# Turned attention scores over 99 rows of the array in place of 128, and no rows of zeros under the queries

## The chip, the cores and the metric

The kernel runs on one core of one Trainium2 chip. The metric is device time of one execution in microseconds (us). Before the change the median of three runs is 1045.04 us, the lowest 1035.89 and the highest 1047.79.

## The reference, cut to what matters

Two decoder-like layers work on `x` (16 sequences, 112 rows, 256 features) with a context of 375 rows for each sequence. The first layer is a masked cross attention with layer norms and a mixture of experts. The second layer is the one that the change touches: a cross attention with 16 heads of 16 features, without a mask, and a small linear layer behind it.

```python
def _L1_xattn_ref(queries, keys, values, Wq, Wk, Wv, Wo):
    q = split_heads(queries @ Wq.T)          # 16 sequences, 16 heads, 112 x 16
    k = split_heads(keys @ Wk.T)             # 16 sequences, 16 heads, 375 x 16
    v = split_heads(values @ Wv.T)
    scores = einsum('bhqd,bhkd->bhqk', q, k) * scale
    attn = softmax(scores, axis=-1)
    ctx = einsum('bhqk,bhkd->bhqd', attn, v)
    return ctx ... @ Wo.T
x = x + _L1_xattn_ref(_layernorm(x), ctx_1024, ctx_1024, ...)
x = x + _L1_ffn_ref(_layernorm(x), W, b, V_r, C)
```

## The kernel before, in words

The first layer and its experts fill the span up to about 650 us; nothing in them is touched. Then comes `layer1`. It treats the 16 sequences ("batches", `b`) one behind the other, in groups of four (`i`), and each batch has 16 heads.

Queries and keys are each cut into three bf16 parts whose sum is nearly the f32 value. Six products of parts are enough, and six blocks of 16 features lie under one another, so that one matmul over `DEPTH` = 96 rows gives the score of one head. The keys of a batch lie in `kst` (128 rows, four slots of batches, 16 heads, 378 places), and the queries of a group in `qst` (128 rows, two slots of groups, 16 heads, 448 places). Both come by DMA from DRAM (`load_keys`, `load_queries` on ScalarE's queue).

Each score is computed twice. `scores` multiplies the queries (stationary, 96 x 112) by the keys (moving, 96 x 375), and VectorE reads only the row maxima out of it (`maximum`, L1472). The negated maxima are cut into three bf16 parts, turned over by the TensorE (`maxima_T`, L1719), copied to `mT` by VectorE (L1491) and written by SyncE's DMAs (`maxima`, L1346) into rows 96, 97 and 98 of `qst`. `transposed` (L1733) then computes the turned scores with the maximum already taken off: the stationary operand is a piece of `kst` with 128 keys, the moving one the 112 queries of a head, and rows 96 to 98 of `kst` hold ones, so that the three parts of the negated maximum are added by the matmul itself. ScalarE takes the exponential (`exps`, L1619), and `outputs` (L1741) multiplies by the values.

`transposed` takes all 128 rows of both tensors. Rows 99 to 127 of `qst` must therefore hold zeros and rows 96 to 127 of `kst` ones. ScalarE fills them: `under_keys(slot)` (L1589) for the four slots of keys and `below_queries(slot)` (L1593) for the two slots of queries. Each is one activation over 32 partitions. The order on ScalarE is written out by hand: 

```python
under_keys(0)
below_queries(0)
turned_over("q", 0)
queries(0)
scaled(1, range(G))
store_queries(0)
load_queries(0)
below_queries(1)
for slot in range(1, 4):
    under_keys(slot)
```

After these come the batches. SyncE's `maxima(b)` waits for the copy `mT` and for `below0` or `below1`, the semaphores of the two fills of `qst`. TensorE waits for the maxima's rows and for `under0` to `under3` before the turned scores of a batch. The stream of TensorE is also fixed by hand: while batch b is being turned and multiplied by values, the plain scores of batch b + 2 are interleaved with it, two heads at a time, each pair behind VectorE's maximum of the pair before.

Of the kernel before, what the change touches and what calls it, by code (L numbers as in the profile page):

```python
# [13 lines left out]
ACT = mybir.ActivationFunctionType  # L14

P = 128
B, S, D = 16, 112, 256
K = 375
KC = 125
NKC = K // KC  # L20
KP = (NKC - 1) * KC + P
# [3 lines left out]
GS = G * S  # L25
E, SE, H = 8, 2, 512
HM = H // P
NH, HD = 16, 16
# [1231 lines left out]
def layer1(nc, ctx, dram, out, x_res, weight1, weight2, slots, ps, bank, ident, ones, always, new_semaphore):  # L1260
# [5 lines left out]
    def sem(name):  # L1266
        return new_semaphore(name)

    DEPTH = 3 * 2 * HD
    QUAD = 4  # L1270
    yscr, kscr, vscr, qscr = (dram[n] for n in ("yscr", "kscr", "vscr", "qscr"))
    wq1 = sb("wq1", [P, C, D])
    wo1 = sb("wo1", [P, C, D])
# [13 lines left out]
    kst = sb("kst", [P, 4, NH, KP], BF16)  # L1287
    qst = sb("qst", [P, 2, NH, GS], BF16)
# [11 lines left out]

    s = {n: sem("d_" + n) for n in (
        "weights_in", "y_in0", "y_in1", "y_in2", "y_in3", "wf_ps", "wf_ready", "identb_ready", "under0", "under1", "under2", "under3",
        "below0", "below1", "dve", "pool", "half_ready", "scaled", "added", "mixed", "mv_ready", "rstd_ready", "xh_ready",
        "xT_ps", "xT_ready", "q_ps", "q1_ready", "q_read", "q2_ready", "q3_ready", "q_out", "qs_in0", "qs_in1",
        "k_in0", "k_in1", "k_in2", "k_in3", "v_in0", "v_in1", "s_ps", "s_max", "m_ready", "mT_ps", "mT_ready",
        "mrow_in0", "mrow_in1", "st_ps", "p_ready", "pv_ps", "outT_ready", "out_ps", "heads_ready", "o_ps", "x3_ready", "bf_added",
        "f_ps", "res_ready", "res_out0", "res_out1", "res_out2", "res_out3")}
# [23 lines left out]
    @block.sync  # L1331
    def _(sp):
        for dst, name in ((wq1, "wq1_t"), (wo1, "wo1_t"), (wf, "wf_t")):
            sp.dma_start(dst[:], dram[name].rearrange("(c p) n -> p c n", p=P)).then_inc(s["weights_in"], 16)
        for dst, name in ((vrT, "vr_t"), (cfT, "cf_t")):
            sp.dma_start(dst[:], dram[name]).then_inc(s["weights_in"], 16)

        sp.dma_start(bf_b[:], dram["bf"].rearrange("(o n) -> o n", o=1).to_broadcast([S, D])).then_inc(s["weights_in"], 16)

        def maxima(b):  # L1340
            i, j = divmod(b, G)
            sp.wait_ge(s["mT_ready"], b + 1)

            sp.wait_ge(s[f"below{i % 2}"], 1)
            for k in range(3):
                sp.dma_start(qst[DEPTH + k:DEPTH + k + 1, i % 2, :, j * S:(j + 1) * S], mT[k * NH:(k + 1) * NH, b % 2, :]).then_inc(s[f"mrow_in{b % 2}"], 16)  # L1346

        def results(i):
            for j in range(G):
                sp.wait_ge(s["res_ready"], i * G + (j + 1))  # L1350
                sp.dma_start(out[i * G + j], res[:, j, :]).then_inc(s[f"res_out{j}"], 16)

        maxima(0)
        for b in range(B):
            i, j = divmod(b, G)
            if b + 1 < B:
                maxima(b + 1)
            if j == 3 and i:
                results(i - 1)
        results(NG - 1)  # L1360
        for j in range(G):
            sp.wait_ge(s[f"res_out{j}"], 16 * NG)
# [221 lines left out]
    @block.scalar  # L1584
    def _(a):
        A = nc.scalar.activation

        def under_keys(slot):
            A(kst[DEPTH:P, slot, :, :].rearrange("p h t -> p (h t)"), ones[DEPTH:P, 0:1].to_broadcast([P - DEPTH, NH * KP]),  # L1589
              ACT.Copy).then_inc(s[f"under{slot}"], 1)  # L1590

        def below_queries(slot):
            A(qst[DEPTH:P, slot, :, :].rearrange("p h t -> p (h t)"), ones[DEPTH:P, 0:1].to_broadcast([P - DEPTH, NH * GS]),  # L1593
              ACT.Copy, scale=0.0).then_inc(s[f"below{slot}"], 1)

        def turned_over(what, i):
            for c in range(C):
                a.wait_ge(s["xT_ps"], TURNS[what, i] * C + (c + 1))
                A(xhT[:, c, :], bank[c][:, 0:GS], ACT.Copy).then_inc(s["xT_ready"], 1)  # L1599

        def queries(i):
            for m in range(C):
                a.wait_ge(s["q_ps"], i * C + (m + 1))
                if m == 0 and i:

                    a.wait_ge(s["q_out"], i * 16)
                A(qa[:, 0, m, :], bank[2 + m][:, 0:GS], ACT.Copy, scale=0.25).then_inc(s["q1_ready"], 1)

        def scaled(i, js):
            for j in js:  # L1610
                b = i * G + j
                a.wait_ge(s[f"y_in{j}"], (i + 1) * 32)
                for k, w in enumerate((weight1, weight2)):
                    A(yg[:, b, k, :], yg[:, b, k, :], ACT.Copy, scale=w[:, b:b + 1]).then_inc(s["scaled"], 1)

        def exps(b, q):
            for k in range(NKC):
                a.wait_ge(s["st_ps"], (b * 4 + q) * NKC + (k + 1))
                A(pT[:, q % 2, k, :], bank[4 + k][0:KC, 0:QUAD * S], ACT.Exp).then_inc(s["p_ready"], 1)  # L1619

        def keep_outputs(b):
            a.wait_ge(s["pv_ps"], b + 1)
            A(outT[:].rearrange("p q t -> p (q t)"), bank[7][:, 0:GS], ACT.Copy).then_inc(s["outT_ready"], 1)

        def load_keys(b):
            to = kst[:, b % 4, :, :].rearrange("p h t -> p (h t)")
            parts = kscr[b].rearrange("s (d g) x -> (s d) (g x)", d=HD)
            for first, n in ((0, 3), (3, 2), (5, 1)):
                a.dma_start(to[first * HD:(first + n) * HD, :], parts[0:n * HD, :]).then_inc(s[f"k_in{b % 4}"], 16)

        def store_queries(i):
            a.wait_ge(s["q3_ready"], i + 1)
            a.dma_start(qscr[i].rearrange("s p x -> p s x"), qa[:].rearrange("p s c t -> p s (c t)")).then_inc(s["q_out"], 16)

        def load_queries(i):
            a.wait_ge(s["q_out"], (i + 1) * 16)
            for r, k in enumerate((0, 0, 0, 1, 1, 2)):
                a.dma_start(qst[r * HD:(r + 1) * HD, i % 2, :, :].rearrange("p h t -> p (h t)"),
                            qscr[i, k].rearrange("(d g) x -> d (g x)", d=HD)).then_inc(s[f"qs_in{i % 2}"], 16)

        def load_values(b):
            a.dma_start(vt[:, b % 2, :, :, :].rearrange("p c h d -> p (c h d)"), vscr[b]).then_inc(s[f"v_in{b % 2}"], 16)

        for b in range(4):
            load_keys(b)
            if b < 2:
                load_values(b)
        under_keys(0)
        below_queries(0)
        turned_over("q", 0)  # L1650
        queries(0)
        scaled(1, range(G))
        store_queries(0)
        load_queries(0)
        below_queries(1)
        for slot in range(1, 4):
            under_keys(slot)
        for b in range(B):
            what, i = blocks_in(b)
            exps(b, 0)  # L1660
            if b:
                keep_outputs(b - 1)
                if b + 1 < B:
                    load_values(b + 1)
            if b % G == 1 and b // G + 1 < NG:
                store_queries(b // G + 1)
            exps(b, 1)
            exps(b, 2)
            if b % G == 1 and b // G + 1 < NG:
                load_queries(b // G + 1)  # L1670
            if what is not None:
                turned_over(what, i)
            exps(b, 3)
            if b + 4 < B:
                load_keys(b + 4)
            if what == "q":
                queries(i)
            j, ahead = b % G, b // G + 2
            if j >= 2 and ahead < NG:
                scaled(ahead, range(2 * (j - 2), 2 * (j - 2) + 2))  # L1680
        keep_outputs(B - 1)
        turned_over("o", NG - 1)
        turned_over("f", NG - 1)

    @block.tensor
    def _(t):
        mm = nc.tensor.matmul
# [38 lines left out]
        def transposed(b, q):  # L1726
            i, j = divmod(b, G)
            for k in range(NKC):
                if b or q:

                    t.wait_ge(s["p_ready"], (b * 4 + (q - 1)) * NKC + (k + 1))
                for h in range(QUAD):
                    last = mm(bank[4 + k][:, h * S:(h + 1) * S], kst[:, b % 4, QUAD * q + h, k * KC:k * KC + P],  # L1733
                              qst[:, i % 2, QUAD * q + h, j * S:(j + 1) * S], start=True, stop=True)
                last.then_inc(s["st_ps"], 1)

        def outputs(b, q):
# [44 lines left out]
        for b in range(B):  # L1782
            what, i = blocks_in(b)
# [207 lines left out]
```

## Time and profile before

| | before |
|---|---|
| median of 3 runs, us | 1045.04 |
| lowest and highest, us | 1035.89, 1047.79 |
| profiled execution, us | 1043.29 |
| its span, first to last instruction, us | 1041.7 |
| TensorE busy in the span, us | 825.4 |
| VectorE, ScalarE, GpSimd busy, us | 467.3, 304.5, 240.2 |
| mean granted TensorE clock | 0.903 |

Times of the trace count from the start of the span. Busy time of an engine is the time in which it has an instruction under way; matmuls overlap, so the busy time of a group is less than its number times the duration of one. The granted clock is 1.0 at 2.4 GHz and 0.5 at 1.2 GHz; values between are means over a stretch that holds both.

### The profile page before, as it was taken

Reading aid. Unit: us, or ns where it says so; the run is one execution under the profiler, and the core shown is the slowest. Engines: PE = TensorE matmul, PEld = TensorE weight load, DVE = VectorE, ACT = ScalarE, POOL = GpSimd, SP = SyncE. Lnnn points to the kernel's source line nnn. Section 1 sums busy time; section 2 is a strip of 40 time slices with the busy share of each in tenths; the row PEclk is TensorE's granted clock in tenths of the full one; section 3 lists DMA queues with packets and bytes.
Section 4 is the critical chain, followed back from the end, with each engine's and each line's share of the span. In section 5 each row is a group of like instructions: output and inputs, shape, how many; then the busy total and the mean of one; then the engine's idle time right before and its main releaser. Section 6 shows DMA issues by size and latency. Waiting matters only on the chain. (4 is left out here: it accounts for less than half of the span.)

```text
span 1041.7 us, 15125 instructions
## 1 busy us (share of the span) xinstructions
PE 825.4 (79%) x5142; PEld 536.2 (51%) x5143; DVE 467.3 (45%) x1083; ACT 304.5 (29%) x547; POOL 240.2 (23%) x298
## 2 busy tenths in 40 slices
PE   6857998999798979899999998003584868878985
PEld 4644565557464645565566555001153546556663
DVE  2527572464246432243444343004553845756732
ACT  1213212311321211122222222042742634533641
POOL 5624331404003330011111111206030241211011
PEclk8989999999999989999999999556577968998998
DMA  8777435215307646255544543395247567585410
GB/s 222 213 226 227 109 99 161 85 59 158 91 1 251 226 131 215 65 145 158 151 145 145 157 151 86 62 184 130 27 103 131 129 141 119 119 148 108 106 35 18
DMA packets 70234, 136.42 MB, mean 131 GB/s; under 512 B 10001, under 2 KB 49298, under 8 KB 68258
## 3 DMA queue, kind: packets, MB, share of 16 engines
q1 hardware_dynamic: 54656, 81.18, 25.2%
q10 hardware_dynamic: 7586, 33.96, 16.6%
q0 software_dynamic: 7936, 20.52, 7.8%
q8 instruction: 36, 0.59, 0.3%
q14 instruction: 20, 0.16, 0.1%
HBM read 104.57 MB, written 30.89 MB: 130 GB/s over the span
## 5 line engine op out<-in xcount | busy, mean ns | idle before, releaser
L1472 DVE TENSOR_REDUCE mxh<-ps 112x2 f32<-112x750 f32 x128 | 115.4, 933 | 71.4 <-PE ps L1714 56.2
L1217 PE MATMUL ps<-rw,rowsT 128*128 x288 | 134.7, 611 | 2.5 <-ACT rowsT L1177 0.6
L1714 PE MATMUL ps<-kst,qst 96*112 96x375 bf16 x256 | 74.7, 386 | 59.0 <-issue 30.7
L1619 ACT ACTIVATE d_pT<-ps 125x448 f32<-125x448 f32 x192 | 90.5, 548 | 96.3 <-PE ps L1733 76.3
L910 PE MATMUL ps<-x1T,sw 128*128 128x448 f32 x256 | 102.3, 546 | 4.3 <-DVE gluT L433 3.0
L1217 PEld LDWEIGHTS ps<-rw,rowsT 128*128 128x128 f32 x288 | 52.3, 191 | 63.6 <-issue 63.6
L910 PEld LDWEIGHTS ps<-x1T,sw 128*128 128x128 f32 x256 | 47.0, 190 | 49.0 <-issue 38.9
L1714 PEld LDWEIGHTS ps<-kst,qst 96*112 96x112 bf16 x256 | 27.7, 147 | 84.0 <-DVE mxh L1472 36.4
L1232 PE MATMUL ps<-rw,gT 128*128 x288 | 68.1, 379 | 0.8 <-ACT gT L1181 0.8
L1123 POOL DMA_DIRECT2D yscr<-y x36 | 19.6, 544 | 204.4 <-DVE y L1156 204.4
L1232 PEld LDWEIGHTS ps<-rw,gT 128*128 128x128 f32 x288 | 54.6, 190 | 23.3 <-issue 17.8
L1143 DVE TENSOR_TENSOR h<-ps,rb 128x512 f32<-128x512 f32 x36 | 24.9, 692 | 83.4 <-PE ps L1217 83.4
L921 PE MATMUL ps<-sw,gluT 128*112 128x256 f32 x256 | 57.6, 380 | 1.4 <-DVE gluT L433 1.4
L1733 PE MATMUL ps<-qst,kst 128*128 128x112 bf16 x768 | 56.1, 229 | 1.9 <-DMA vt<-vscr 1.3
L937 PE MATMUL ps<-wv,cT 128*125 128x256 f32 x192 | 48.1, 404 | 11.2 <-DVE kr L446 11.2
L1733 PEld LDWEIGHTS ps<-qst,kst 128*128 128x128 bf16 x768 | 48.3, 107 | 12.1 <-issue 3.9
L1741 PE MATMUL ps<-d_pT,vt 125*17 125x112 f32 x1536 | 52.8, 274 | 0.3 <-ACT d_pT L1619 0.3
L921 PEld LDWEIGHTS ps<-sw,gluT 128*112 128x112 f32 x256 | 45.3, 178 | 13.2 <-DVE gluT L433 2.2
L930 PE MATMUL ps<-cT,wk 128*128 128x378 f32 x128 | 45.7, 501 | 7.5 <-issue 5.4
L305 POOL DMA_INDIRECT xg<-xh_moe,places x32 | 30.6, 957 | 84.2 <-DVE places L520 75.3
L433 DVE SCALAR_TENSOR_TENSOR gluT<-ps,sb,silu 128x448 f32<-128x448 f32 x32 | 21.9, 683 | 60.5 <-ACT silu L742 60.4
L937 PEld LDWEIGHTS ps<-wv,cT 128*125 128x125 f32 x192 | 37.6, 199 | 21.8 <-DVE kr L446 15.1
(211 smaller groups left out, 1210.0 us busy)
## 6 DMA issues: line engine op xcount, KB each, us to landing
rb<-in_rb SPq DMA_DIRECT2D x36, 512.0 KB, 3.8
rw<-in_rw SPq DMA_DIRECT2D x24, 512.0 KB, 7.6
kscr<-ka SPq DMA_DIRECT2D x16, 567.0 KB
kst<-kscr ACTq DMA_DIRECT2D x16, 567.0 KB, 12.2
vscr<-va SPq DMA_DIRECT2D x16, 398.4 KB
vt<-vscr ACTq DMA_DIRECT2D x16, 398.4 KB
ctxT<-in_ctx_t SPq DMA_DIRECT2D x16, 378.0 KB
cT<-in_ctx_t SPq DMA_DIRECT2D x16, 378.0 KB, 8.2
```

The source lines that it names most:

```text
L305: pool.indirect_dma_start(out=dram["xg"], out_offset=bass.IndirectOffsetOnAxis(ap=places[0:S, k, b:b + 1], axis=0), in_=xh_moe[:, b, :], i ...
L910: last = mm(bank[up_in(i, m)[k]][:, 0:GS], w[:, e, c, h * P:(h + 1) * P], x1T[:, c, :], start=c == 0, stop=c == C - 1)
L921: last = mm(bank[j % 2][0:S, 0:D], gluT[:, m, j * S:(j + 1) * S], sw3[:, e, h, :], start=m == 0, stop=m == U - 1)
L930: last = mm(ps[:, 2 + m, 0:KP], wk1[:, c, m * P:(m + 1) * P], cT[:, b % 3, c, :], start=c == 0, stop=c == C - 1)
L937: last = mm(bank[2 + k // 2][0:KC, (k % 2) * D:(k % 2 + 1) * D], cT[:, b % 3, c, k * KC:(k + 1) * KC], wv1[:, c, :], start=c == 0, stop=c ...
L1217: last = mm(bank[1 + 2 * q + k], rowsT[:, q, c * P:(c + 1) * P], w[:, e, c, :], start=c == 0, stop=c == C - 1)
L1232: last = mm(bank[6][:, 0:D], gT[:, q, m * P:(m + 1) * P], rw3[:, e, m, :], start=m == 0, stop=m == HM - 1)
L1472: V.tensor_reduce(mxh[:, 2 * g:2 * g + 2], ps[0:S, 2 * (g % 2):2 * (g % 2) + 2, 0:K], axis=AX_X, op=ALU.max).then_inc(s["s_max"], 1)
L1619: A(pT[:, q % 2, k, :], bank[4 + k][0:KC, 0:QUAD * S], ACT.Exp).then_inc(s["p_ready"], 1)
L1714: last = mm(bank[2 * (g % 2) + k][0:S, 0:K], qst[0:DEPTH, i % 2, h, j * S:(j + 1) * S], kst[0:DEPTH, b % 4, h, 0:K], start=True, stop=True)
L1733: last = mm(bank[4 + k][:, h * S:(h + 1) * S], kst[:, b % 4, QUAD * q + h, k * KC:k * KC + P], qst[:, i % 2, QUAD * q + h, j * S:(j + 1) * ...
L1741: last = mm(bank[7][32 * h:32 * h + HD + 1, q * S:(q + 1) * S], vt[:, b % 2, k, QUAD * q + h, :], pT[:, q % 2, k, h * S:(h + 1) * S], star ...
```

## The change

`transposed` takes rows 0 to 98 of both operands (`ROWS_T`), 96 rows of parts and the three of the maximum, where it took 128. The ones under the keys are written to three rows only. The two fills with zeros under the queries are gone, and with them their two semaphores and SyncE's wait for them. The number of matmuls, their columns and their order stay.

```diff
+    ROWS_T = DEPTH + 3
...
             sp.wait_ge(s["mT_ready"], b + 1)
-
-            sp.wait_ge(s[f"below{i % 2}"], 1)
...
         def under_keys(slot):
-            A(kst[DEPTH:P, slot, :, :].rearrange("p h t -> p (h t)"), ones[DEPTH:P, 0:1].to_broadcast([P - DEPTH, NH * KP]),
+            A(kst[DEPTH:ROWS_T, slot, :, :].rearrange("p h t -> p (h t)"), ones[DEPTH:ROWS_T, 0:1].to_broadcast([ROWS_T - DEPTH, NH * KP]),
               ACT.Copy).then_inc(s[f"under{slot}"], 1)
-
-        def below_queries(slot):
-            A(qst[DEPTH:P, slot, :, :].rearrange("p h t -> p (h t)"), ones[DEPTH:P, 0:1].to_broadcast([P - DEPTH, NH * GS]),
-              ACT.Copy, scale=0.0).then_inc(s[f"below{slot}"], 1)
...
         under_keys(0)
-        below_queries(0)
         turned_over("q", 0)
...
         load_queries(0)
-        below_queries(1)
         for slot in range(1, 4):
             under_keys(slot)
...
                 for h in range(QUAD):
-                    last = mm(bank[4 + k][:, h * S:(h + 1) * S], kst[:, b % 4, QUAD * q + h, k * KC:k * KC + P],
-                              qst[:, i % 2, QUAD * q + h, j * S:(j + 1) * S], start=True, stop=True)
+                    last = mm(bank[4 + k][:, h * S:(h + 1) * S], kst[0:ROWS_T, b % 4, QUAD * q + h, k * KC:k * KC + P],
+                              qst[0:ROWS_T, i % 2, QUAD * q + h, j * S:(j + 1) * S], start=True, stop=True)
```

On ScalarE, from the first fill to the first exponentials, the order before is this (`d_` marks tensors of the second layer, x3 is three of a kind):

```order
L1589 ACTIVATE kst<-ones 32x6048
L1593 ACTIVATE qst<-ones 32x7168
L1599 ACTIVATE d_xhT<-ps 128x448 x2
L1607 ACTIVATE qa<-ps 128x448 x2
L1614 ACTIVATE yg<-yg,weight 112x256 x8
L1633 DMA qscr<-qa 128x3x896
L1638 DMA qst<-qscr 16x7168 x6
L1593 ACTIVATE qst<-ones 32x7168
L1589 ACTIVATE kst<-ones 32x6048 x3
L1619 ACT_TABLE_LOAD
L1619 ACTIVATE d_pT<-ps 125x448 x9
```

The same stretch of ScalarE in the changed kernel:

```order
L1588 ACTIVATE kst<-ones 3x6048
L1594 ACTIVATE d_xhT<-ps 128x448 x2
L1602 ACTIVATE qa<-ps 128x448 x2
L1609 ACTIVATE yg<-yg,weight 112x256 x8
L1628 DMA qscr<-qa 128x3x896
L1633 DMA qst<-qscr 16x7168 x6
L1588 ACTIVATE kst<-ones 3x6048 x3
L1614 ACT_TABLE_LOAD
L1614 ACTIVATE d_pT<-ps 125x448 x9
```

Two activations are gone from it, and the four others write 3 partitions instead of 32; the rest stands in the same order.

## Rows read from the trace of the kernel before

**Rows 1.** The page: busy time by engine, and the granted clock in 40 slices.
```profile
PE 825.4 (79%) x5142; PEld 536.2 (51%) x5143; DVE 467.3 (45%) x1083; ACT 304.5 (29%) x547; POOL 240.2 (23%) x298
...
PEclk8989999999999989999999999556577968998998
```

**Rows 2.** Windows, by stage: length, busy of each engine (instructions), clock, DMA.
```profile
650.00:706.00 56.00, 0.00 (x0) 0.00 (x0) 5.26 (x14) 11.30 (x2) 8.15 (x10) 0.54 0.67 120
706.00:755.00 49.00, 22.18 (x56) 9.71 (x57) 23.68 (x47) 28.32 (x17) 16.87 (x20) 0.57 0.35 77
755.00:1018.00 263.00, 208.19 (x2796) 146.06 (x2793) 156.82 (x309) 115.47 (x248) 48.53 (x51) 0.88 0.56 113
```

**Rows 3.** Timeline of TensorE, 814 to 826 us: start, busy, line, [idle before <- releaser].
```profile
814.61 0.23 PE L1719 MATMUL ps<-identb,mparts 112*48 112x112 bf16 x1 [0.39 <-DVE mxh L1472]
815.46 0.65 PE L1750 MATMUL ps<-ident,outT 128*112 128x128 f32 x4 [0.62 <-DVE mxh L1472]
815.94 0.48 PE L1714 MATMUL ps<-kst,qst 96*112 96x375 bf16 x2
...
817.06 0.53 PE L1714 MATMUL ps<-kst,qst 96*112 96x375 bf16 x2
817.42 0.75 PE L1733 MATMUL ps<-qst,kst 128*128 128x112 bf16 x12
```

**Rows 4.** Windows: that same batch.
```profile
814.61:825.70 11.09, 9.78 (x166) 6.47 (x166) 9.50 (x16) 7.56 (x19) 2.87 (x4) 1.00 0.67 146
```

**Rows 5.** Timeline of ScalarE, 678 to 756 us.
```profile
678.28 5.24 ACT L1589 ACTIVATE kst<-ones 32x6048 bf16<-32x6048 f32 x1 [31.27 <-issue]
683.42 6.15 ACT L1593 ACTIVATE qst<-ones 32x7168 bf16<-32x7168 f32 x1
710.88 0.54 ACT L1599 ACTIVATE d_xhT<-ps 128x448 f32<-128x448 f32 x1 [21.30 <-PE ps L1693]
...
724.35 2.67 ACTq L1638 DMA_DIRECT2D qst<-qscr  x6
727.06 6.17 ACT L1593 ACTIVATE qst<-ones 32x7168 bf16<-32x7168 f32 x1 [6.03 <-issue]
733.14 15.48 ACT L1589 ACTIVATE kst<-ones 32x6048 bf16<-32x6048 f32 x3
748.64 1.28 ACT L1619 ACT_TABLE_LOAD   x1
755.42 1.42 ACT L1619 ACTIVATE d_pT<-ps 125x448 f32<-125x448 f32 x3 [5.50 <-PE ps L1733]
```

**Rows 6.** Waits of SyncE's queue: who waited, us in total, times, longest.
```profile
SPq L1346 <- DVE mT L1491: 266.9, 16, 59.8
SPq L1344 <- ACT qst L1593: 18.0, 1, 18.0
```

**Rows 7.** Timeline of TensorE, start of the layer and first turned scores.
```profile
737.10 1.47 PE L1714 MATMUL ps<-kst,qst 96*112 96x375 bf16 x4 [19.97 <-issue]
...
757.18 1.33 PE L1733 MATMUL ps<-qst,kst 128*128 128x112 bf16 x12
```

**Rows 8.** The turned scores as a group: busy us, mean ns | idle before.
```profile
L1733 PE MATMUL ps<-qst,kst 128*128 128x112 bf16 x768 | 56.1, 229 | 1.9 <-DMA vt<-vscr 1.3 <-DVE res L1514 0.2
```

**Rows 9.** Durations in ns, min/median/max, by line and shape.
```profile
L1733 PEld LDWEIGHTS ps<-qst,kst x768: 95/98/153, 754.5 to 1015.4; 128*128 128x128 bf16 x192
L1733 PE MATMUL ps<-qst,kst x768: 210/213/301, 754.8 to 1015.4; 128*128 128x112 bf16 x192
...
L1714 PEld LDWEIGHTS ps<-kst,qst x256: 126/130/218, 737.1 to 993.4; 96*112 96x112 bf16 x128
L1714 PE MATMUL ps<-kst,qst x256: 320/325/563, 737.1 to 993.6; 96*112 96x375 bf16 x128
...
L1719 PEld LDWEIGHTS ps<-identb,mparts x16: 98/99/115, 748.5 to 995.9; 112*48 112x48 bf16 x16
```

**Rows 10.** Windows of 3 us, the columns of rows 2; first and last return to full clock.
```profile
739.00:742.00 3.00, 2.81 (x7) 1.02 (x8) 2.76 (x4) 3.00 (x1) 0.00 (x0) 0.50 0.00 0
...
757.00:760.00 3.00, 2.70 (x23) 1.64 (x25) 1.85 (x4) 1.42 (x3) 0.00 (x0) 0.50 0.00 0
...
763.00:766.00 3.00, 2.99 (x49) 2.33 (x47) 1.79 (x2) 1.53 (x4) 0.00 (x0) 0.94 0.00 0
...
1006.00:1009.00 3.00, 3.00 (x27) 2.26 (x28) 0.95 (x3) 0.00 (x0) 0.00 (x0) 1.00 0.15 43
```

More of the change, by code:

```diff
@@ L1302, in layer1 @@
         "weights_in", "y_in0", "y_in1", "y_in2", "y_in3", "wf_ps", "wf_ready", "identb_ready", "under0", "under1", "under2", "under3",
-        "below0", "below1", "dve", "pool", "half_ready", "scaled", "added", "mixed", "mv_ready", "rstd_ready", "xh_ready",
+        "dve", "pool", "half_ready", "scaled", "added", "mixed", "mv_ready", "rstd_ready", "xh_ready",
         "xT_ps", "xT_ready", "q_ps", "q1_ready", "q_read", "q2_ready", "q3_ready", "q_out", "qs_in0", "qs_in1",
```

## The prediction

> **What bounds the kernel now.** I read the page first [rows 1]. TensorE is the busiest engine (79% of the span), and its granted clock is near full until the second layer begins, where it drops to about half and comes back slowly. Then I cut the span by stage [rows 2], because the change touches only what lies behind 650 us. Three stretches matter. From 650 to 706 us TensorE does nothing: the layers are handed over. From 706 to 755 us the second layer starts up, with TensorE busy for 22 of 49 us. From 755 to 1018 us the sixteen batches run, with TensorE busy for 208 of 263 us, against 157 for VectorE and 115 for ScalarE; so TensorE is the engine to watch there.
>
> In a batch that no transfer disturbs [rows 3, 4] the period is 11.09 us, TensorE is busy for 9.78 and VectorE for 9.50. TensorE's gaps are short (0.39 and 0.62 us) and both are waits for VectorE's maxima. The two are thus nearly in balance, TensorE a little ahead: a longer matmul shows almost in full, a shorter one would soon run into the maxima.
>
> **The change part by part.**
>
> *The first fill of zeros*, 6.15 us on ScalarE from 683.42 us [rows 5]. Behind it ScalarE stands idle for 21.30 us, until TensorE has turned the first norms at 710.88 us. SyncE's 18.0 us wait for this fill [rows 6] ends there too, long before the first plain scores start at 737.10 us [rows 7]. If the fill goes, the idle time becomes 27.5 us. Cost on the path: 0.
>
> *The second fill*, 6.17 us from 727.06 us [rows 5]. Behind it stand the three fills of ones (15.48 us), the loading of the exponential's table (1.28 us), and then 5.50 us of idle time, until TensorE delivers the first turned scores. Without the fill this chain ends 6.2 us earlier and the idle time becomes 11.7 us. What holds the turned scores is the chain over the plain scores: TensorE waits 19.97 us for the queries' loads, until 737.10 us [rows 7], and then the maxima of the first batch, their turning and SyncE's DMAs follow. None of these waits for the fill, whose queue had already issued the six query loads (they begin at 724.35 us) when it began. On the path: 0. The bounds: it can't cost anything, since ScalarE only loses work, and it could give at most its own 6.2 us, if the write into `qst` slowed the loads that run at the same time. I take 0.
>
> *The four fills of ones over 3 partitions.* The fill of 6048 columns takes 5.16 us (15.48 / 3) and the one of 7168 columns 6.17 us [rows 5]: 0.85 and 0.86 ns a column, so the columns set the time, and they stay. No row shows one over few partitions; the bounds are 0 and all 15.48 us saved, and both lie in front of the same 5.50 us of idle time, so either is worth 0 on the path.
>
> *SyncE's wait for the fills* was satisfied at 690 us. All 16 of its other waits are for `mT` [rows 6]. Worth 0.
>
> *768 matmuls over 99 rows instead of 128*, 56.1 us busy [rows 8]. There is no matmul over 99 rows in the trace, but one over 96: the plain scores. At full clock a matmul of 375 columns over 96 rows takes 325 ns and one of 112 columns over 128 rows 213 ns [rows 9]. Take off the columns at 2.4 GHz (156.3 and 46.7 ns): 168.7 ns stay with 96 rows and 166.3 with 128. Fewer rows save nothing. Nor in the pace: a pair of plain scores takes 0.48 us [rows 3], so the second starts 480 - 325 = 155 ns behind the first, which is its columns alone; twelve turned scores take 0.75 us, a step of (750 - 213) / 11 = 49 ns, which is 46.7 plus 2. Bounds for one matmul: nothing, and the 2.4 ns by which the row over 96 rows is longer (1.8 us for all 768, were it not hidden by the overlap). I take 0.
>
> *768 weight loads of 99 rows and 128 columns instead of 128 and 128.* Here the trace leaves a gap. A bf16 load of 112 rows and 48 columns takes 99 ns, one of 96 rows and 112 columns 130 ns [rows 9]: 0.48 ns a column, whatever the rows. On that line 128 columns would take 138 ns, and the full 128 x 128 load takes 98. So the full bf16 load is a fast one, and no row of it shows whether it is so by its 128 columns or by its 128 rows. If by the columns, nothing changes: 0. If by the rows, each load becomes up to 40 ns longer: at least 62 ns a step by the columns' slope (128 x 0.48) against the step of 49 now, which is 13 ns x 768 = 10 us; at most about the 50 ns by which a pair of scores is longer when its load is not covered (0.53 against 0.48 us, [rows 3]), which is 38 us. I take 0, because every other duration in rows 9 goes by columns.
>
> The Trainium skill ("TensorE: Matmul & The Clock Gate", section "Weight-path perf modes", on fast weight load) says that the fast load is on when the number of weights is 128 and the type isn't FP32; the section on LDWEIGHTS counts weights by columns and says that the contraction rows don't matter. By that rule the sum stays at 0. The same skill ("Trainium Kernel Development and Optimization", "Best Practices") asks for tiles of 128 partitions, which speaks against the change; it gives no price, and with the fast load kept by the columns none is left here.
>
> **The sum** is 0 against the profiled execution (1043.29 us, span 1041.7), which lies 1.75 us under the median of the runs. I give 1044, between the two.
>
> **The rivals.**
>
> *Slower, the fast load is lost* (chance 6%). Its place is the turned scores of every batch, and the point from which it decides is whether the chip wants 128 rows for it. For it: a fast load over fewer rows is not to be seen in the trace. Against: durations go by columns elsewhere. Price: the difference between the two bf16 loads, 130 - 98 = 32 ns, for 768 loads is 25 us, nearly all on the path, because TensorE's slack is 1 us in a batch of 11: about 1069 us, and by the bounds 1054 to 1082.
>
> *Slower, the clock comes back later* (4%). Matmuls that use fewer rows would be granted the full clock later. For it: from 737 us TensorE is up to 94% busy with scores over 96 rows and stays at 0.50, and only behind 760 us, with turned scores and outputs mixed in, does it reach 0.94 [rows 10]. Against: the turned scores take only 2.4 of 11 us in a batch (48 x 49 ns). In my windows of 3 us the clock comes back nine times between 763 and 1009 us. Were each return 3 us later, half of 3 us would be lost nine times: 13.5 us, so 1058 us.
>
> *Faster, the fills were in the way after all* (7%). ScalarE's writes into `qst` would slow the loads into it that TensorE awaits for 19.97 us. Price: up to 6.2 us, 1038 us. Against: they write other partitions than the loads do, and TensorE's wait ends 3.9 us after the fill.
>
> *The kernel does not do what it says*: the order on the engines shows two activations gone and the same matmuls, so I give it nothing.
>
> **How the numbers follow.** That nothing on the path moves has 83%. A measurement of this kernel can tell a change of about 1%, 10.4 us, from none. The three runs before lie 12 us apart, so the second layer's transfers alone move an execution by about 1%, and a median of few can fall some us to either side. Forecast and the faster rival both stay inside 1%, but for that scatter: I put 8% on more than 1% faster (5 of the 83, 3 of the 7) and, with the two slower rivals and 1% of scatter, 11% on slower; 81% stays within. The range of 1035 to 1050 us leaves out the two slower rivals (10%) and about 10% of scatter beyond the extremes of the runs seen; it takes in the 6.2 us of the faster rival and the 2 us of the longer matmul.
>
> **What would show it.** In the profile after, the group of turned scores should read 99*128, with the load at 98 ns and the matmul at 213 ns in the median, 768 of each, and twelve of them in 0.75 us. ScalarE's busy time should be 12.3 us lower, with about 11.7 us of idle time before the first exponentials. An undisturbed batch should still take 11.1 us. The first plain scores should start 20 us behind the queries' product, as now. The forecast is wrong if the load reads near 130 ns (first rival), if the clock in the batches is below 0.88 in the mean (second), or if the scores start earlier than 19 us behind the queries' product (third).

## The result, and the profile after

Over 20 runs each the changed kernel takes 1046.93 us in the median (1040.16 to 1055.77) and the kernel before 1042.41 (1035.89 to 1047.79). The ratio is 1.0041 with a 95% interval of [1.0021, 1.006]. The change costs about 4 us. Ratios and mean clocks, here and below, leave out the few runs that lie more than 1.5% above the fastest run of their kernel, here the one of 1055.77 us. The result lies inside the range given and inside 1%, but it is clear of the scatter, and the forecast had said that nothing on the path would move.

The profiled execution took 1050.79 us (span 1049.2), against 1043.29 before. It is slower than the median, so its 7.5 us overstate the loss; the places are what it is good for. The busy times and the clock in 40 slices, from the page of the changed kernel:

```profile
PE 833.9 (79%) x5142; PEld 540.8 (52%) x5143; DVE 467.5 (45%) x1083; ACT 292.6 (28%) x545; POOL 240.5 (23%) x298
...
PEclk8978999999999999999999999555576989898998
```

Against [rows 1], ScalarE lost the 11.9 us of the two fills. TensorE has as many instructions as before and is busy 8.5 us longer. The turned scores themselves, by line (now L1726), with the min/median/max durations in ns:

```profile
L1726 PEld LDWEIGHTS ps<-qst,kst x768: 95/98/153, 757.5 to 1022.9; 99*128 99x128 bf16 x192
L1726 PE MATMUL ps<-qst,kst x768: 210/213/301, 757.9 to 1023.0; 99*128 99x112 bf16 x192
```

These are the numbers of [rows 9] to the nanosecond. A load of 99 rows and 128 columns is as fast as one of 128 rows, and so is the matmul. ScalarE's timeline around the second fill's old place (start, busy, line, idle before):

```profile
680.67 5.24 ACT L1588 ACTIVATE kst<-ones 3x6048 bf16<-3x6048 f32 x1 [32.06 <-issue]
712.95 0.55 ACT L1594 ACTIVATE d_xhT<-ps 128x448 f32<-128x448 f32 x1 [27.04 <-PE ps L1686]
...
730.14 15.50 ACT L1588 ACTIVATE kst<-ones 3x6048 bf16<-3x6048 f32 x3 [6.02 <-issue]
745.66 1.28 ACT L1614 ACT_TABLE_LOAD   x1
758.48 1.42 ACT L1614 ACTIVATE d_pT<-ps 125x448 f32<-125x448 f32 x3 [11.53 <-PE ps L1726]
```

Both fills are gone and both times of idling grew by nearly their length, by 5.7 us for a fill of 6.15 (21.30 to 27.04 us) and by 6.0 for one of 6.17 (5.50 to 11.53) [rows 5]. A fill of 3 partitions takes 5.2 us, as one of 32 did. TensorE at the start of the layer, from its timeline:

```profile
714.29 5.92 PE L1693 MATMUL ps<-d_xhT,wq 128*128 128x448 f32 x8 [0.63 <-ACT d_xhT L1594]
740.16 1.47 PE L1707 MATMUL ps<-kst,qst 96*112 96x375 bf16 x4 [19.94 <-issue]
...
757.86 1.33 PE L1726 MATMUL ps<-qst,kst 99*128 99x112 bf16 x12
```

The wait for the loads is 19.94 us, as in [rows 7]; from the first plain scores to the first turned ones it is 17.70 us in both traces. And an undisturbed batch at full clock (windows: length, busy of TensorE, its loads, VectorE, ScalarE, GpSimd, clock, DMA):

```profile
818.79:829.87 11.08, 9.89 (x165) 6.43 (x165) 9.49 (x16) 7.55 (x19) 2.88 (x4) 1.00 0.70 145
```

11.08 us, against 11.09 in [rows 4]. So every duration is unchanged, and yet time is lost. The place shows when one looks at the return to the full clock. Windows of 3 us, of the kernel before and then of the changed one:

```profile
755.00:758.00 3.00, 3.00 (x26) 2.55 (x24) 2.86 (x8) 1.62 (x4) 0.00 (x0) 0.50 0.02 5
...
761.00:764.00 3.00, 3.00 (x30) 2.26 (x30) 1.32 (x2) 1.42 (x3) 0.00 (x0) 0.61 0.01 1
764.00:767.00 3.00, 2.90 (x47) 2.30 (x40) 1.56 (x3) 1.74 (x5) 0.00 (x0) 1.00 0.00 0
```

```profile
758.00:761.00 3.00, 3.00 (x26) 2.55 (x25) 2.86 (x8) 1.57 (x4) 0.00 (x0) 0.50 0.00 0
...
767.00:770.00 3.00, 3.00 (x34) 2.28 (x33) 1.58 (x2) 0.38 (x1) 0.00 (x0) 0.50 0.00 0
770.00:773.00 3.00, 3.00 (x21) 2.19 (x20) 0.94 (x1) 2.01 (x5) 0.00 (x0) 0.86 0.35 60
```

The last column but two is the granted clock. Before, the full clock returned 26 us behind the first plain scores (737.10 us), after, 31 us behind them (740.16 us), though the same instructions stand there in the same order. The stage of the batches reads:

```profile
755.00:1018.00 263.00, 211.06 (x2650) 146.87 (x2653) 158.94 (x310) 109.51 (x235) 48.63 (x51) 0.85 0.56 112
```

0.85 instead of 0.88 [rows 2]: in the same 263 us TensorE got through 2650 matmuls instead of 2796, in part because the changed kernel entered the window 3 us later. From the first plain score to the end of the last turned one, TensorE had 80.8 us at the low clock before and 92.1 after; 4.5 of the 11.3 us more lie ahead of the first return, the others behind it. 11.3 us at half speed lose up to 5.6 us of work; the stretch grew by 4.5 us (278.5 to 283.0). The rest of the 7.5 us is 1.85 us that was already there when the layer began (its first matmul at 708.70 against 706.85 us, ahead of all that the change touches) and 1.2 us in the start-up, most of it the queries' product (5.92 against 4.90 us), which the change doesn't touch either.

### The profile page after: what moved, and what is told of

It is laid out like the page before. It is cut to its first block and busy times, and to the rows that moved or that the text cites. A ratio compares the mean times of both kernels' runs of the same rounds, so it can differ in the third digit from the quotient of the medians.

```text
span 1049.2 us, 15107 instructions
## 1 busy us (share of the span) xinstructions
PE 833.9 (79%) x5142; PEld 540.8 (52%) x5143; DVE 467.5 (45%) x1083; ACT 292.6 (28%) x545; POOL 240.5 (23%) x298
## 5 line engine op out<-in xcount | busy, mean ns | idle before, releaser
L1726 PE MATMUL ps<-qst,kst 99*128 99x112 bf16 x768 | 56.5, 230 | 2.2 <-DMA vt<-vscr 1.6
L1734 PE MATMUL ps<-d_pT,vt 125*17 125x112 f32 x1536 | 55.1, 281 | 0.3 <-ACT d_pT L1614 0.3
L1726 PEld LDWEIGHTS ps<-qst,kst 99*128 99x128 bf16 x768 | 48.6, 108 | 12.8 <-issue 4.1
L1748 PE MATMUL ps<-cfT,vrT 32*128 32x256 f32 x4 | 2.1, 670 | 58.0 <-DMA bf_b<-in_bf 58.0
```

The costliest lines, as they stand in the source:

```text
L1726: last = mm(bank[4 + k][:, h * S:(h + 1) * S], kst[0:ROWS_T, b % 4, QUAD * q + h, k * KC:k * KC + P], qst[0:ROWS_T, i % 2, QUAD * q + h, j ...
L1734: last = mm(bank[7][32 * h:32 * h + HD + 1, q * S:(q + 1) * S], vt[:, b % 2, k, QUAD * q + h, :], pT[:, q % 2, k, h * S:(h + 1) * S], star ...
```

## The experiments

Two theories stood against each other. **Clock**: matmuls over fewer rows are granted the full clock less, though each takes the same time at a given clock. **Fills**: taking ScalarE's fills away moves something in time. A third was that any rebuilt kernel lies a few tenths of a per cent off. Each kernel was compared with the kernel before side by side, on the same chip. The table is read with the texts below it. Clocks are means over the timed runs; their standard error is 0.0008 to 0.0015 (0.0023 for e8), and for the kernel before 0.0005 to 0.0008.

| run | turned rows | plain rows | ratio, 95% interval | clock before | clock |
|---|---|---|---|---|---|
| e6 | 127 | 96 | 1.0017 [0.9993, 1.0041] | 0.9058 | 0.9048 |
| e5 | 112 | 96 | 1.0022 [0.9996, 1.0047] | 0.9058 | 0.9022 |
| e1 | 99 | 96 | 1.0048 [1.0016, 1.008] | 0.9057 | 0.8992 |
| e16 | 99 | 96 | 1.0011 [0.9983, 1.0038] | 0.9013 | 0.8967 |
| e4, the change | 99 | 96 | 1.0031 [1.0001, 1.006] | 0.9057 | 0.9016 |
| e18, the change | 99 | 96 | 1.0079 [1.0048, 1.011] | 0.9011 | 0.8935 |
| e7 | 128 | 65 | 1.0056 [1.003, 1.0081] | 0.9058 | 0.8997 |
| e8 | 99 | 65 | 1.0145 [1.0102, 1.0189] | 0.9058 | 0.8763 |
| e14 | 99 | 65 | 1.0155 [1.0127, 1.0183] | 0.9013 | 0.8698 |
| e3 | 128 | 128 in 8 batches | 1.0016 [0.9991, 1.004] | 0.9057 | 0.9057 |
| e11 | 128 | 128 | 1.0011 [0.9976, 1.0047] | 0.9013 | 0.9038 |
| e15 | 99 | 128 | 1.0035 [1.0014, 1.0056] | 0.9013 | 0.8983 |
| e13 | 128, 29 of zeros only | 96 | 1.0008 [0.9992, 1.0025] | 0.9013 | 0.8988 |
| e2 | 128 | 96 | 1.0018 [0.9994, 1.0043] | 0.9057 | 0.9046 |
| e17 | 128 | 96 | 1.0014 [0.9992, 1.0037] | 0.9011 | 0.9009 |
| e9, idle work | 128 | 96 | 1.0043 [1.0015, 1.0071] | 0.9013 | 0.9049 |
| e10, the change, idle work | 99 | 96 | 1.001 [0.9992, 1.0028] | 0.9013 | 0.9036 |
| e12, idle work | 128 | 128 | 1.0033 [1.0013, 1.0054] | 0.9013 | 0.9094 |

**Rows alone, fills alone, and the change again.** The edit of e1 and e16 is the matmul's alone, the fills stay:

```diff
-last = mm(..., kst[:, b % 4, ...], qst[:, i % 2, ...])
+last = mm(..., kst[0:99, b % 4, ...], qst[0:99, i % 2, ...])
```

> The kernel before with one edit: the turned scores take 99 rows, all fills stay. The change measured 1.0041 of before [1.0021, 1.006]. Clock theory (matmuls over fewer rows are granted the full clock less): this run shows the whole loss, ratio 1.003 to 1.006, with a mean granted clock in the timed runs some 0.005 below that of before. Fill theory (the loss comes from the fills that are gone, by a shift in time of ScalarE's work): ratio 1.000, clock as before. Scatter theory (any rebuilt kernel may lie some tenths of a per cent away): no foretelling, the run of the change itself in this call should then move too.

> Turned scores over 99 rows, all fills kept, a second time: if rows set the loss, 1.002 to 1.007 and a clock 0.004 to 0.008 below that of before. Near 1.000 with the clock as before would mean that the first result was scatter.

In e2 and e17 the matmuls keep 128 rows and only the second fill leaves its place:

```diff
         below_queries(0)
+        below_queries(1)
         turned_over("q", 0)
...
         load_queries(0)
-        below_queries(1)
```

> The kernel before with one edit: the second fill of zeros stands ahead of the first turned norms, in ScalarE's idle time, and not behind the query loads; the matmuls keep 128 rows. Clock theory: ratio 1.000 and the clock as before. Fill theory: the second fill is gone from its place as in the change, so ratio 1.004.

> 128 rows, the second fill of zeros moved into ScalarE's idle time, a second time. If the fills are worth nothing: 0.999 to 1.001, clock as before. If they carry part of the loss: 1.002 or more again.

> The changed kernel once more, beside the others. If its loss is a property of the kernel: ratio 1.002 to 1.006. If it was scatter of the day or of the chip: near 1.000.

> The changed kernel, a third comparison. If the loss is the kernel's, by the rows and the clock: 1.002 to 1.006 with a clock 0.004 to 0.007 below that of before.

The change was slower in all three comparisons, in e18 by more than expected. Weighted by their intervals they give 1.0047, about [1.003, 1.006]. The rows alone give 1.0027, [1.001, 1.005], over two comparisons that agree in the clock (0.0065 and 0.0046 lower, both as the clock theory asked) and less well in the time: e16 by itself, 1.0011, does not differ from the kernel before. The second fill moved (e2, e17) leaves the clock where it was (0.001 and 0.000 lower) and gives 1.0016, about [1.000, 1.003], e17 between the two ranges expected: the fill may cost up to 3 us or nothing, and by what, no run shows. This tests one of the removals only: no run leaves out the first fill, or writes the ones over 3 partitions, at 128 rows. That part stays open.

Rebuilding alone does not explain the change: its clock fell in e4 and in e18, and that of e17 did not. But a part of each ratio may come from it. No kernel here measured below the one before, not even those meant to be neutral or faster (1.0008 to 1.0018 for e2, e3, e11, e13 and e17), and none was rebuilt without an edit to show what that costs. So a ratio of 1.001 or 1.002 by itself is no evidence about its edit. The change's 1.0047 lies above that, and so do those of e7, e8 and e14.

The size of the loss fits the clock. Among the runs of the kernel before on one chip, one with a clock lower by 0.001 takes 0.4 to 0.8 us longer (a straight line through the runs of each of the five chips). By the line of their own chip the lower clocks of e1, e16, e4 and e18 are worth 5, 2, 3 and 4 us, where 5, 1, 3 and 8 were measured, and those of e7, e8 and e14 (below) 3, 16 and 14 us, where 6, 15 and 16 were. A correlation is no proof, since whatever makes TensorE wait can lower the clock too; but the sizes leave little for a second cause, e18 apart.

**More and fewer rows.** e5 and e6 are e1 with 112 and 127 in the place of 99. e7 takes rows from the plain scores instead, and e8 and e14 from both:

```diff
-qst[0:DEPTH, i % 2, h, ...], kst[0:DEPTH, b % 4, h, 0:K]
+qst[0:65, i % 2, h, ...], kst[0:65, b % 4, h, 0:K]
```

> The kernel before with the turned scores over 112 rows, all fills kept. With 99 rows alone the ratio was 1.0048 [1.0016, 1.008] and the mean granted clock 0.8992 against 0.9057. Clock theory in proportion to the rows: half the loss, ratio 1.002, clock near 0.902. Clock theory with a step (only the full 128 rows count as full): the whole loss, 1.004 to 1.005. Theory that the number of rows does not matter: 1.000.

> The kernel before with the turned scores over 127 rows, all fills kept. In proportion to the rows: ratio 1.000 (a thirtieth of the loss). Step at the full array: 1.004 to 1.005, clock near 0.899. Loss of the fast weight load by rows would show as a load of over 98 ns, which 99 rows did not show.

> The kernel before with the plain scores over 65 rows instead of 96, the turned scores over 128; only the maxima, which any value near them serves, lose their smallest parts. A batch has 6,000 columns of plain scores and 5,376 of turned ones, so 31 rows fewer here weigh about as much as the 29 of the change. Clock theory in proportion to rows: ratio 1.004 to 1.006, clock near 0.899. Step at 128 rows, which the plain scores never had: 1.000. Rows don't matter: 1.000.

> Turned scores over 99 rows and plain scores over 65, all fills kept. Clock theory in proportion: the two losses add, ratio 1.008 to 1.011, clock near 0.893. Step at 128: 1.004 to 1.005, as with the turned scores alone. Rows don't matter: 1.000.

> Turned scores over 99 rows, plain ones over 65, a second time. If the loss of 1.0145 [1.0102, 1.0189] is the kernel's: 1.010 to 1.019 with a clock some 0.02 to 0.03 below that of before. If it was of six runs on one chip: near 1.005.

With 127, 112 and 99 rows the clock falls by 0.0010, 0.0036 and 0.0065 (0.0046 in e16): as far as the standard errors can tell in proportion, and not in a step at the full array. The times of e5 and e6 alone could not decide that. The plain scores, which never had 128 rows, cost about as much per row (0.0061 for 31 rows). Both together cost about three times what one does in time, and more in the clock (0.0295 and, on another chip, 0.0315 lower, where the sum is 0.0126): more than the sum that was expected. In the trace of e8, by line and in ns:

```profile
L1734 PEld LDWEIGHTS ps<-qst,kst x768: 95/98/153, 744.3 to 1014.1; 99*128 99x128 bf16 x192
L1734 PE MATMUL ps<-qst,kst x768: 209/213/301, 744.6 to 1014.1; 99*128 99x112 bf16 x192
```

and its windows, first the stage of the batches, then a piece inside it, and behind it such a piece in the trace of e14:

```profile
755.00:1018.00 263.00, 222.46 (x2714) 156.52 (x2703) 151.08 (x299) 111.51 (x239) 48.58 (x51) 0.80 0.56 113
```

```profile
789.70:804.00 14.30, 14.30 (x151) 9.84 (x151) 7.15 (x10) 4.92 (x11) 0.00 (x0) 0.50 0.48 98
```

```profile
803.00:817.00 14.00, 14.00 (x147) 9.65 (x151) 6.90 (x10) 4.70 (x10) 0.00 (x0) 0.50 0.42 89
```

Durations at the full clock are the old ones, but TensorE works 14 us without a gap at 0.50. Behind the first plain scores the longest such piece of unbroken work at the low clock is 5 to 7 us in the four traces with 128 and 96 rows (before, e2, e13, e17), 7 and 8 us with 99 and 96 (e16, e1), 9 us in the three of the change and in e7, and 14 in both of 99 and 65. The fourth batch, at the full clock throughout in the kernel before, spends 7 of its 14 us at 0.50 in e8 and in e14. That would explain a loss that is more than a sum: each wait that lets the clock fall has a longer way back behind it. It is a reading of single traces, and no run tests it by itself.

A single profile says less than the means. The first return came 26, 26 and 21 us behind the first plain scores with 128 turned rows (before, e2, e17), 26 and 21 us with 99 rows and the fills kept (e1, e16), and 31 us in all three profiles of the changed kernel. So the return at the start may need the missing fills as well as the missing rows; the mean clocks, with e4 0.0041 and e18 0.0076 down against 0.0065 and 0.0046 for the rows alone, do not tell the two apart.

**Rows given instead of taken.** e3 gives the plain scores of 8 batches 128 rows and moves all fills ahead of the first turned norms, e11 gives 128 rows to all of them (a DMA writes zeros over the old maxima first), and e15 does so beside the change's 99 rows. e13 keeps 128 rows but puts zeros in rows 99 to 127 of the keys as well.

```diff
+a.dma_start(qst[DEPTH:DEPTH + 3, i % 2, :, :]..., qst[DEPTH + 3:DEPTH + 6, i % 2, :, :]...)
...
-qst[0:DEPTH, i % 2, h, ...], kst[0:DEPTH, b % 4, h, 0:K]
+qst[:, i % 2, h, ...], kst[:, b % 4, h, 0:K]
```

> The kernel before, turned scores over 128 rows as there, and the plain scores of the first 8 batches also over 128 rows (rows 96 to 127 hold zeros in the queries then, so the sums stay); all fills stand ahead of the first turned norms. Clock theory: more rows in use, so the clock comes back earlier at the start of the layer and the kernel is 1 to 5 us faster (ratio 0.995 to 0.999), clock up by some 0.003. Fill theory and the rule that rows cost nothing: ratio 1.000, within 1 us for the fills that are moved.

> The kernel before with the plain scores over 128 rows in all 16 batches; a seventh DMA in each group of query loads writes zeros over the old maxima, so the sums stay. Clock theory in proportion to rows, upward too: clock 0.910 to 0.913, ratio 0.994 to 0.997. If only a loss of rows counts (the batches already run at full clock most of the time): 1.000. The added DMA: 0 to 1 us.

> Turned scores over 99 rows as in the change, plain scores over 128 in all batches (with the DMA that writes zeros over old maxima); fills kept. 32 rows more on 6,000 columns against 29 fewer on 5,376: if rows of all matmuls count alike, the loss is made up, ratio 0.999 to 1.001, clock as before. If only the turned scores' rows count: 1.003 to 1.006, clock 0.005 lower.

> The kernel before, turned scores over all 128 rows, but with zeros in rows 99 to 127 of the keys too (before: ones there, zeros in the queries), filled in ScalarE's idle time. If the number of rows taken counts: as before, ratio 1.000, clock as before. If the cells that hold something other than zero count: the loss of 99 rows, ratio 1.003 to 1.005, clock 0.005 lower.

More rows do not buy time. e11's clock is 0.0025 higher, two standard errors, and its time no shorter. In the traces of e11, e3 and e15 the first return of the full clock comes 19 to 20 us behind the first plain scores, against 26 before; but e17 and e13, with 96 rows there, have it at 21 and 20 us, so this is no sign of an effect. TensorE waits for VectorE's maxima between most pairs of that stretch, so a faster clock has little to give there; that is argued, not shown. e15 did not make up for the missing rows: its clock is 0.0030 lower than before, within the errors of e16's 0.0046, and its time is as long as the change's. e13 is unclear: its clock lies 0.0025 lower, about half of what 99 rows cost and two standard errors, and its time is that of before within 0.0017. Whether the rows count or what stands in them stays open.

**A clock held up by idle work.** e9 and e10 are the kernel before and the changed one with 60 matmuls of ones by ones where TensorE waits for the loads; e12 is e11 with them.

```diff
         queries(0)
+        for _ in range(60):
+            mm(bank[6][:, 0:P], ones[:], ones[:], start=True, stop=True)
         arrived(0)
```

> The kernel before with 60 idle matmuls (f32, 128 x 128 of ones, into a bank that nobody reads) between the queries' product and the first plain scores, where TensorE waits 20 us for loads. Clock theory: the clock is full when the loads land, the first scores and turned scores run at 2.4 GHz instead of 1.2, and the kernel gains the low-clock share of the stretch from 737 to 763 us, of which TensorE alone sets some 8 us: 2 to 5 us (ratio 0.995 to 0.998). If the clock were a mere sign of something else (transfers): 1.000, or slower if the idle matmuls end behind the loads.

> The changed kernel with the same 60 idle matmuls. The changed kernel alone gave 1.0031 [1.0001, 1.006] and 1.0041 [1.0021, 1.006]. If the change loses at the first return to the full clock only, the idle matmuls give all of it back: ratio as e9_warm, 0.995 to 0.998. If it loses in the batches too: between, 0.998 to 1.002.

> Both: plain scores over 128 rows and the 60 idle matmuls. Clock theory: the gains of e9_warm and e11_scores128_all add, ratio 0.990 to 0.995, clock over 0.913. Otherwise 1.000.

None gains time. e9 (1.0043) and e12 (1.0033) miss what was expected and are slower; e10 (1.001) falls into the second range given for it, for a change that loses in the batches too, but that range rested on a gain in e9 that did not come. The timeline of e9 shows why there is no gain:

```profile
715.80 13.56 PE L1761 MATMUL ps<-ones 128*128 128x128 f32 x120
737.27 1.47 PE L1714 MATMUL ps<-kst,qst 96*112 96x375 bf16 x4 [7.90 <-issue]
```

The idle work ended 7.90 us before the loads landed, the clock had fallen again, and the first four scores take 1.47 us as in [rows 7]. The mean clock rose (0.9049 against 0.9013), but where it is worth nothing: from 715.80 to 729.36 us it was 1.00 against 0.74 in the kernel before, and in the wait behind it 0.64 against 0.50, which alone is 0.004 in the mean. So the mean clocks of kernels with idle work can be compared only with each other. There the change costs nothing that shows: e10 is no slower than e9, and its clock is lower by 0.0013, less than the errors of the two. That does not fit a loss of 0.5% in every setting, and it was not followed up. Why e9 is slower, with its first scores 0.17 us later than in [rows 7], was not found. No version beats the kernel before.

## Why the prediction was wrong

**The fills and SyncE's wait**, costed at 0: the idle times grew by nearly their length. The runs with the second fill moved allow a cost of 0 to 3 us, so the step is neither refuted nor settled to the last microsecond. The faster rival (fills in the way of the loads, up to 6.2 us) is refuted: TensorE's wait for the loads is 19.94 us after and 19.97 before. The ones over 3 partitions take what they took over 32 (5.24 us for the first of them in both traces).

**The weight loads**, the gap in the trace, costed at 0: right. The load takes 98 ns with 99 rows as with 128; the slower rival of the lost fast load falls. The Trainium skill ("TensorE: Matmul & The Clock Gate", "Weight-path perf modes") says that the fast load goes by the number of weights and the type; these traces agree, since at 128 columns and bf16 the rows change nothing (98 ns with 99, 112, 127 and 128).

**The matmuls over 99 rows**, costed at 0, "fewer rows save nothing": the duration was right (213 ns, a batch in 11.08 us), and the step still failed. This is the step that made the forecast wrong. It held duration and pace at a given clock to be the whole price. The rows had a second one, the granted clock, and every matmul beside them pays it: with the rows as the only edit it fell by 0.0065 and 0.0046, and the time rose by 0.27% (0.1 to 0.5%) of the 0.47% that the whole change costs. What is left between the two is not settled.

The rival "the clock comes back later" named the mechanism and got 4%. The sign that it gave came true, a clock in the batches below 0.88 (0.85), and those of the two other rivals did not. Its price was 13.5 us, from nine returns each 3 us later, 27 us more at the low clock; the profile shows 11.3 us more, and over the runs the change cost 4 to 5 us. The first return was 4 to 5 us later in the profile of the changed kernel than in that of the kernel before, but not in those of the rows alone. Its counter-argument, that the turned scores take only 2.4 of 11 us in a batch, did not carry: a longer way back after a wait is enough, if the reading of e8 and e14 is right. Its argument in favour did not carry either. [rows 10] has TensorE 94% busy with scores over 96 rows and still at 0.50; in e11 the same scores over 128 rows keep it as busy (2.81 of 3 us, from 740 to 743 us), at 0.50 too. So the rival was right about the rows without evidence for them, and none of the rows shown from the trace before gives any.

**The range** held the median and the 1% bound was right; that nothing would move was wrong by 0.4%. The range laid the scatter between runs to the second layer's transfers. No run shows that; what the runs show is that the longer ones have the lower clock.

## What to carry to other kernels

A matmul over fewer rows took exactly as long here at a given clock, so leaving out rows of zeros saved nothing on TensorE, and it cost clock for everything around it. Where a kernel's granted clock is well below 1 in a stage that TensorE bounds, look at what an edit does to the returns to full clock before calling it free, and compare mean clocks over many runs: here they separated kernels that the times alone could not. They can mislead where an edit puts work into a stretch in which TensorE would wait.

## What the runs showed of the hardware

The mean granted clock fell with the rows in use: 0.9058 with 128 turned rows, 0.9048, 0.9022 and 0.8992 with 127, 112 and 99, and 0.8763 with 99 and 65 (0.9013 to 0.8967 and 0.8698 on another chip), while load and matmul of the turned scores stayed at 98 and 213 ns in the median of every trace. Whether it goes by the rows taken or by what stands in them is open (e13). TensorE without a gap is no sign of a full clock: in e8 and e14 it ran at 0.50 through 14 us of unbroken work. An activation over 3 partitions took 5.2 us for 6048 columns, the same as over 32. Chips differed by 1.3% (the kernel before at 1029.0 us in the median on two and at 1041.8 to 1042.5 on three), more than any effect here but that of both cuts together, so only comparisons on the same chip count.
